# Reordering the attention slot: scores ahead of queries and keys, row maximum earlier, projection last

## The reference

```python
q = (layernorm(x) @ Wq)                      # heads of 64
k, v = ctx @ Wkv                             # heads of 64
atten = softmax(q @ k.T * SCALE)             # per head, 128 x 128
x = x + (atten @ v) @ Wproj + bproj
logits = layernorm(x) @ gate_w.T             # 8 experts, softmax, top 2
expert_out = silu(tokens @ expert_w.T + expert_b)
mixed = sum of the two chosen expert_out * their probability
x = x + mixed @ combine_w.T
```

## Time and profile before

| | |
|---|---|
| runs, us | 1871.58, 1879.7, 1884.8 (median 1879.7) |
| profiled execution, us | 1882.66 |
| its span, us | 1880.2 |
| busy: PE, DVE, ACT, POOL | 84%, 66%, 56%, 48% of the span |
| steps | 256, first S at 29.1 us, last S at 1654.2 us |
| median time of a key transfer from issue to landing | 2.5 us |
| mean granted TensorE clock | 0.946 of full speed |

### The profile page before, as it was taken

How to read it: one execution, slowest core, us unless ns; L and a number is a source line. 1 busy time by engine, 2 the same in 40 slices (tenths; PEclk the granted TensorE clock), 3 DMA queues, 4 the chain that set the end, 5 groups by cost and what they waited for, 6 DMA issues and landing times.

```text
span 1880.2 us, 39451 instructions
## 1 busy us (share of the span) xinstructions
PE 1579.7 (84%) x11835; PEld 1489.1 (79%) x11835; DVE 1247.1 (66%) x3090; ACT 1049.8 (56%) x2904; POOL 911.8 (48%) x1213
## 2 busy tenths in 40 slices
PE   4788888888899999888999999879999998965664
PEld 4677777787789999888898888878998887865554
DVE  6567676767677777677777777667777776643222
ACT  4555555555566666565666666656666665642232
POOL 3535554545454545454555555555555555453042
PEclk9999999999899999999999999989999998987677
DMA  6632223333466666333667776336667744676785
GB/s 208 231 84 77 74 78 79 79 80 79 125 196 205 196 200 190 88 96 109 181 203 209 207 208 192 97 110 194 206 202 211 205 122 121 192 239 208 234 277 169
DMA packets 187210, 303.79 MB, mean 162 GB/s; under 512 B 24725, under 2 KB 119162, under 8 KB 186490
## 3 DMA queue, kind: packets, MB, share of 16 engines
q1 hardware_dynamic: 174714, 267.71, 48.7%
q0 software_dynamic: 12288, 33.57, 5.8%
HBM read 164.06 MB, written 70.01 MB: 124 GB/s over the span
## 4 chain that ended last, share of the span: by engine, by line
PE 41%; ACT 15%; DVE 13%; issue 12%; POOL 12%; DMA 4%; SPq 3%; another core or an unknown queue 0%; POOLq 0%; ACTq 0%; DVEq 0%
PE gen_ps L490 10%; PE proj_ps L490 10%; PE s_ps L490 9%; ACT probs L724 6%; POOL o_s_lo L1141 5%; DVE neg_max L881 5%; PE qk_ps L490 4%; ACT stage L697 4%; PE o_ps L490 3%; POOL o_s_hi L1139 3%; ACT pT_s_hi L697 2%; PE pT_ps L528 2%; POOL sorted_x L1149 2%; PE gen_ps L578 1%; DMA sorted_y<-stage 1%
## 5 line engine op out<-in xcount | busy, mean ns | idle before, releaser
L724 ACT ACTIVATE probs<-s_ps,neg_max 128x128 f32<-128x128 f32 x1024 | 292.8, 369 | 535.5 <-DVE neg_max L881 491.7
L1139 POOL CAST o_s_hi<-stage 128x256 fp32r<-128x256 f32 x256 | 102.0, 398 | 620.8 <-ACT stage L697 620.4
L490 PE MATMUL proj_ps<-wproj_s_hi,o_s_hi 128*128 128x256 f32 x512 | 165.2, 323 | 160.9 <-POOL o_s_lo L1141 150.3
L888 DVE TENSOR_REDUCE sums<-probs 128x4 f32<-128x512 f32 x256 | 175.3, 685 | 157.2 <-ACT probs L724 156.6
L881 DVE TENSOR_REDUCE neg_max<-s_ps 128x4 f32<-128x512 f32 x256 | 177.0, 691 | 146.6 <-PE s_ps L490 119.8
L1130 POOL TENSOR_TENSOR probs<-probs,inv_sums 128x512 f32<-128x512 f32 x256 | 266.2, 1040 | 9.3 <-DVE inv_sums L890 9.3
L490 PEld LDWEIGHTS proj_ps<-wproj_s_hi,o_s_hi 128*128 128x128 f32 x512 | 98.1, 192 | 203.5 <-POOL o_s_lo L1141 196.8
L490 PE MATMUL s_ps<-k_s,qk_s 128*128 128x256 f32 x1536 | 235.5, 291 | 16.3 <-DMA k_s<-qk_s 15.5
L839 DVE TENSOR_TENSOR pT_s_lo<-pT_ps,pT_s_hi 128x512 fp32r<-128x512 f32 x256 | 177.1, 692 | 87.5 <-ACT pT_s_hi L697 85.4
L490 PEld LDWEIGHTS s_ps<-k_s,qk_s 128*128 128x128 f32 x1536 | 209.6, 197 | 18.3 <-DMA k_s<-qk_s 18.3
L1141 POOL TENSOR_TENSOR o_s_lo<-stage,o_s_hi 128x256 fp32r<-128x256 f32 x256 | 187.3, 732 | 21.1
(11 more groups left out here) (169 smaller groups left out, 4707.8 us busy)
## 6 DMA issues: line engine op xcount, KB each, us to landing
w_block<-expert_table SPq DMA_DIRECT2D x163, 512.0 KB
k_s<-qk_s SPq DMA_DIRECT2D x512, 128.0 KB, 2.5
stage<-sorted_x SPq DMA_DIRECT2D x163, 128.0 KB
sorted_y<-stage SPq DMA_DIRECT2D x163, 128.0 KB
x_raw<-in_x SPq DMA_DIRECT2D x32, 256.0 KB
c_raw<-in_ctxT SPq DMA_DIRECT2D x32, 256.0 KB
stage<-in_x SPq DMA_DIRECT2D x32, 256.0 KB
x_kept<-x SPq DMA_DIRECT2D x32, 256.0 KB
```

The costliest lines, as they stand in the source:

```text
L490: mm = pe.matmul(out_ap, l, r, start=start and n == 0, stop=stop and n == len(terms) - 1, skip_group_check=skip)
L724: last = act.activation(probs[p % 2][:, k, :], s_ps[:, k * P:(k + 1) * P], ACT.Exp, bias=neg_max[p % 2][:, k:k + 1])
L888: dve.tensor_reduce(sums[p % 2][:, :], probs[p % 2][:, :, :], AX_X, ALU.add).then_inc(sums_done, 1)
L1139: pool.tensor_copy(hi[:, :, :], o_full).then_inc(o_hi, 1)
```

## The change

Nothing is computed differently. Within a slot the calls are put in another order on three engines.

- TensorE: T(n-1), **S(n+1)**, QK(n+2), mid jobs, A(n-1), **P(n-2)**, late jobs. S moves from behind P to ahead of QK; P moves from ahead of S and A to behind A.
- ScalarE: the cast of step n - 1 (`pT`) stands ahead of the copies of step n - 2 (`attended`).
- VectorE: max(n+1) stands straight behind sum(n); `add_residual` (only in u = 2) ahead of it; pT_lo(n-1) and all the others behind it.

```diff
@@ tensor
                 general(s, "early")
+                if u < 7 and now:
+                    scores(i, u + 1)
+                if u == 7 and nxt:
+                    scores(i + 1, 0)
                 if u < 6 and now:
                     queries_keys(i, u + 2)
...
                 general(s, "mid")
+                if u == 0 and before:
+                    attend(i - 1, 7)
+                if u > 0 and now:
+                    attend(i, u - 1)
                 if u < 2 and before:
                     project(i - 1, 6 + u)
                 if u >= 2 and now:
                     project(i, u - 2)
-                if u < 7 and now:
-                    scores(i, u + 1)
...
@@ scalar
+                if u == 0 and before:
+                    pT(i - 1, 7)
+                if u > 0 and now:
+                    pT(i, u - 1)
                 if u < 2 and before:
                     attended(i - 1, 6 + u)
...
@@ vector
                     inverse(i, u)
+                if u == 2 and before:
+                    add_residual(i - 1)
+                if u < 7 and now:
+                    row_max(i, u + 1)
+                if u == 7 and nxt:
+                    row_max(i + 1, 0)
                 if u == 0 and before:
                     pT(i - 1, 7)
```

More of the change, by code:

```diff
@@ L802, in _ @@
                     attended(i, u - 2)
[L803 to L806, removed]
                 if s - 2 in plan.turn:
@@ L1056, in _ @@
                     pT(i, u - 1)
-                if u == 2 and before:
-                    add_residual(i - 1)
                 general(s, "early")
@@ L1068, in _ @@
                 general(s, "mid")
[L1069 to L1072, removed]
                 if u == 0 and nxt:
```

## The result

| | before | changed |
|---|---|---|
| time, median (lowest to highest) | 1879.38 us (1871.58 to 1884.8) | 2168.65 us (2166.16 to 2179.04) |
| ratio, 95% interval | | 1.155 (1.150 to 1.161) |
| span of the profiled execution | 1880.2 us | 2167.4 us |
| first S to last S started | 29 to 1653.7 us | 29 to 1933.9 us |

The change costs 289 us, 15.5%. The direction and the mechanism are the forecast ones; the size was put at 210 us. 2168.65 us lies just inside the range, but the ratio, applied to the 1879.7 us that stood before the prediction, gives 2171.6, just above its end of 2170.

A forecast was written before the change was run, and what follows sets the result against it. TensorE was taken as bound by its waits in the loop through o_lo and P. First S 29, plain 898, full 872, hold-ups 36, clock 26, tail 226: span 2087 us, 2090 with 2.5 around it; range 1985 to 2170.

The forecast's parts named there:

- P last removes P's wait and costs nothing: On TensorE, P behind A finds its o_lo done; removes at most 160 us of idle time and costs nothing itself.
- Rival A: Faster: the key transfer stays hidden and a slot becomes TensorE's own work; 1720 us, chance 0.03.
- ScalarE's order, 0: On ScalarE, the cast ahead of the copies delays o_hi by 0.59 us, hidden because P moved back by more.
- VectorE's order, 0 with a bound of 49 us: On VectorE, the early max delays neither pT_lo nor qk_lo; taken as 0, at most 0.4 us in 123 slots.
- S ahead of QK closes a loop of one slot: S, QK, cast, subtraction, key transfer, next S: 3.75 us to the issue, slots of 6.75 us plain, 7.15 full.
- Full slots, 3.4 from issue to S: In full slots, 3.4 us from key-transfer issue to S, against 3.0 in plain ones; 122 x 7.15 = 872 us.
- Rival E: Weight loads delay keys in full slots, 4.0 us from issue, 2163 us; or VectorE delays qk_lo, 49 us; chance 0.07.
- The clock, 26 us: On TensorE, a third of 66 plain slots without a large job lose 1.2 us to half clock: 26 us.
- Rival D: TensorE's clock falls behind nearly every long wait: 120 us instead of 26, 2184 us, chance 0.1.
- The places where SyncE is held up, start 12 and chunk ends 24: SyncE hold-ups beyond the slot: 12 us at the start, 6 us at each of four chunk ends, 36 together.
- The tail: The stretch at the end without attention, 226 us, stays as before.
- rival C: Key transfers always land like the quick ones: 6.6 us in all 255 slots, no clock loss, 1974 us, chance 0.13.

## Why the prediction was right and where it was wrong

Step by step, in us; "before" and "after" are sums from S to S in the two traces.

| | steps | before | forecast | after | miss |
|---|---|---|---|---|---|
| start | 10 | 68.3 | 79.5 | 116.5 | +37 |
| chunk ends | 12 | 92.7 | 108 | 121.1 | +13 |
| plain slots | 112 | 676.4 | 778 | 786.7 | +9 |
| full slots | 121 | 787.2 | 867 | 880.4 | +13 |
| tail, behind the last S | | 226.6 | 226 | 233.5 | +7 |

(The forecast's 6.75 and 7.15 us a slot are spread over the classes, with the 36 us for hold-ups and the 26 for the clock; its whole is 2087 us. The miss is 80 us of 2167.)

**P last removes P's wait and costs nothing.** Right: 3.3 us are left, and alone it gives 6%. Rival A, "the key transfer stays hidden", had the price 1720 us for the same gain; the run gave 1774. Beside these 54 us stand 33 us more of waits for keys, 48.2 us against 15.5.

**ScalarE's order, 0.** Open in the changed kernel, where it was never tried without VectorE's; together they cost 12 to 27 us, where the sum had nothing. It is not free where there is no key loop: 1.3% on top of P last.

**VectorE's order, 0 with a bound of 49 us.** A little too small in the changed kernel, and inside the bound: by the traces qk_lo ended later than its cast allows by 7 us in all over the 121 full slots, 3 us at the chunk ends and under 1 in the plain ones. But the reason given, "done at about 2.2, while qk_lo cannot start before 3.0", is a statement about the loop and not about max: as soon as S stands behind QK the same order costs 0.105 of the time, mostly through A's wait for pT_lo.

**S ahead of QK closes a loop of one slot.** Right, and shown from four sides: it alone makes the loss, two more issues make it longer by about what they take, without the transfer the loss is gone, and the trace shows each link. The loop of a plain slot was put at 6.75 and is 6.5 to 6.6. The mean of 7.02 is above the forecast all the same: in 17 of 112 slots QK was slowed by the lower clock, 23 us in all, and in the mean S stood 3.16 behind the end of qk_lo, not the 2.9 to 3.0 of the undisturbed slots. That comes from 17 slots, most of them close to a chunk end, with 3.4 to 5.7 us. SyncE issued 0.03 us behind qk_lo in each of them; in 12 TensorE then waited for the keys, which landed late, and in 5 no wait stands ahead of S.

**Full slots, 3.4 from issue to S.** The term was a little small: 3.51 in the mean from the end of qk_lo, with 7 us of lower clock and the 7 us of VectorE above added. Rival E's 4.0 was too much. That 3.4 fits is partly luck. It was taken for slower landings, and the landings were about as quick as in the plain slots. In 31 of the 121 full slots S had no wait on record ahead of it: TensorE came from its own work (the S at 1246.03 and at 1253.24 are 7.21 us apart, and TensorE stood still nowhere between them). The 6.2 us that the prediction set against the loop was a mean over slots of unlike length, and where work and loop are so near, the longer of the two counts in each slot.

**The clock, 26 us.** The size was right, 23 in plain slots and 7 in full ones, but not where it falls: 16 more were lost in the first ten slots, all of them at half clock (QK ended 3.6 to 4.0 us behind S, not 2.3), and 9 at the chunk ends. The whole clock term is 55 us. Rival D, "nearly every long wait", was wrong: most waits of 2 us don't bring it.

**The places where SyncE is held up, start 12 and chunk ends 24.** This is the step that failed: the price of SyncE's hold-ups, at the start above all, where 12 us stood for what measured 49. The prediction priced a hold-up by how long S had waited for it before, 9.3 us in one place, although before a whole slot of slack lay over the others. The view to read was SyncE's waits, not TensorE's: keep_expert waited 8 times for GpSimd, 29.0 us in the kernel before and 71.6 after. The row of before, which the prediction didn't read:

```profile
SPq L378 <- POOL w_block L1112: 29.0, 8, 6.5
```

In a loop without slack such a wait counts each time. It measured 37 us above the term (16 of them in the lower clock that the longer waits brought with them), and moving keep_expert gives 33 back. At the chunk ends the 8.7 us of clears stand ahead of the key transfer, and one step there takes 14.6 to 14.9 us instead of 6.6. SyncE's timeline:

```profile
578.67 8.69 SPq L367 DMA_DIRECT2D sorted_x<-zero_rows  x8
587.47 9.78 SPq L359 DMA_DIRECT2D k_s<-qk_s  x4
```

8 us each, 32 in all and more with the clock, where 24 stood in the sum. The clears don't start at once either. SyncE first waits for VectorE's ranking to say which rows to clear, 3.6 us at this place:

```profile
SPq L366 <- DVE clear_at L1010: 17.8, 5, 3.8
```

qk_lo was done at 581.22 there, and its transfer went out at 587.47. No run moved the clears or the ranking, so this part rests on the trace.

**The tail.** The 7 us above need not be an effect of the change: in the thirteen traces the time behind the last S lies between 214 and 235 us, in no order that follows the edits. It rather follows the chip: 229 to 235 us in the four experiments on one chip, 214 to 223 in the seven on the other. The range could have taken this scatter in. It also doesn't hold what it is said to hold: rival C's 1974 us lie below its end of 1985.

## What to carry to other kernels

Before moving a consumer ahead of a producer in one in-order queue, write down the chain from the consumer back to itself, through every engine, queue and transfer, and compare its length with what the engine has to do in a round: a transfer that was hidden a slot ahead becomes the whole round when the consumer of one item stands in front of the producer of the next. Once such a loop is closed, price everything in it by the queues that it passes, not by what the waiting engine had waited for until then: each short wait ahead of the transfer in SyncE's queue now counts in full. And try the parts of a change one at a time; here one part was a gain of 6%, and nearly the whole loss was in one moved call.

## What the runs showed of the hardware

The length of a wait ahead of S did not decide the clock by itself. In the changed kernel S was slowed, wholly or in part (1.2 to 1.65 us instead of 0.98), in none of the 112 slots with a wait below 1.5 us ahead of it, in 3 of 43 between 1.5 and 2.1, 8 of 26 between 2.1 and 2.5, none of 6 between 2.5 and 3, and 19 of 20 above 3. A wait of 1.98 us brought it at one place and 3.67 us didn't at another. The Trainium skill (TensorE: Matmul & The Clock Gate, "HAM oscillation — how this bites in real kernels") tells of loops that start each round throttled; here that holds for the start, where all of the first ten slots were slowed, and not for the plain slots, of which 17 in 112 were.

Splitting a write by rows costs more than its elements: a cast of 128 x 512 in one instruction took 0.59 us, the same elements in two of 64 x 256 and one of 128 x 256 took 0.75 + 0.37 = 1.12, and VectorE's subtraction 0.86 + 0.42 = 1.28 instead of 0.69. A piece of 64 rows took as long as one of 128 with the same columns (0.75 / 2 and 0.37, 0.86 / 2 and 0.42). Four issues of 64 KB instead of two of 128 KB moved the first use back by 1.02 us, while SyncE was busy for 2.38 instead of 1.11 us.
